# A graph network's second pass over its edge counts, with six chunk buffers in place of four

## The reference, cut to what matters

```
def sage_conv(x, edge_index, w_l, b_l, w_r):
    src, dst = (edge_index[0], edge_index[1])
    n = x.shape[0]
    msg_sum = jax.ops.segment_sum(x[src], dst, num_segments=n)
    deg = jax.ops.segment_sum(jnp.ones((src.shape[0],), x.dtype), dst, num_segments=n)
    mean = msg_sum / jnp.maximum(deg, 1.0)[:, None]
    return mean @ w_l + b_l + x @ w_r
h = jax.nn.relu(sage_conv(x, edge_index, w1_l, b1, w1_r))
return sage_conv(h, edge_index, w2_l, b2, w2_r)
```

## Time and profile before

| | |
|---|---|
| time, median of 3 runs | 5765.54 us (5760.69 to 5777.83) |
| span of the profiled execution | 5738.2 us |
| TensorE matmul busy | 3339.7 us (58%) |
| VectorE busy | 3535.7 us (62%) |
| TensorE mean granted clock | 0.733 of full |
| first row of `l1a_end` to first row of `l1b_end` on VectorE | 2585.84 to 2773.69 us |

### The profile page before, as it was taken

One profiled execution on the slowest core, in us unless ns is written; L12 is line 12 of the kernel. 1 busy time (PEld: TensorE's weight loads), 2 busy tenths in 40 slices (PEclk: granted clock), 3 DMA queues, 4 the chain that ended last, 5 costly groups with the idle time before them and its releaser, 6 DMA issues. The chain is left out here.

```text
span 5738.2 us, 59061 instructions
## 1 busy us (share of the span) xinstructions
PE 3339.7 (58%) x14332; PEld 2164.9 (38%) x14332; DVE 3535.7 (62%) x6569; ACT 2184.6 (38%) x3989; POOL 2244.9 (39%) x2086
## 2 busy tenths in 40 slices
PE   5666679999999999798413433325014342433564
PEld 3555534444444444355312323324013232323452
DVE  6999989999999999510214323325135553645676
ACT  4999968887878787300000000000002111111310
POOL 0000023333333333100276777773566666666200
PEclk8999989999999999899655555555555555555556
DMA  2555544444444443697411242210211111111011
GB/s 71 163 163 162 162 134 118 114 118 108 124 104 114 119 109 100 134 195 157 93 37 39 47 90 50 47 45 18 36 28 36 31 36 30 35 31 29 5 38 35
DMA packets 546254, 474.36 MB, mean 83 GB/s; under 512 B 185773, under 2 KB 439736, under 8 KB 545085
## 3 DMA queue, kind: packets, MB, share of 16 engines
q1 hardware_dynamic: 493723, 416.13, 28.6%
q0 software_dynamic: 52288, 55.34, 4.8%
HBM read 351.39 MB, written 119.84 MB: 82 GB/s over the span
## 5 line engine op out<-in xcount | busy, mean ns | idle before, releaser
L813 PE MATMUL l_sum_ps<-arena,sums 125*65 125x500 f32 (+1 forms) x2600 | 1140.8, 577 | 9.9 <-ACT arena L774 4.8
L1711 POOL DMA_INDIRECT l_rows<-table,tile_src x782 | 794.4, 1016 | 406.9 <-issue 212.0
L1126 POOL DMA_INDIRECT l_rows<-hidden_rows,tile_src x782 | 796.3, 1018 | 326.4 <-issue 231.8
L692 POOL COPY arena<-arena 125x750 f32<-125x750 f32 (+1 forms) x400 | 540.4, 1355 | 893.8 <-PE l_count_ps L802 855.7
L758 ACT ACTIVATE arena<-arena,far_left 125x750 f32<-125x750 f32 (+1 forms) x800 | 713.4, 939 | 282.7 <-DVE arena L711 282.7
L711 DVE SCALAR_TENSOR_TENSOR arena<-arena,far_past 125x750 f32<-125x750 f32 (+1 forms) x800 | 803.8, 1045 | 16.5 <-DMA arena<-score_rows 16.5
L722 DVE SCALAR_TENSOR_TENSOR arena<-arena,l_count_ps 125x750 f32<-125x750 f32 (+1 forms) x800 | 735.4, 960 | 96.5 <-ACT arena L763 51.9
L1187 PE MATMUL l_sum_ps<-l_rows,l_hot 128*125 x1612 | 359.9, 414 | 747.0 <-issue 678.7
L1153 DVE TENSOR_TENSOR sums<-sums,l_sum_ps 125x64 f32 x806 | 178.5, 222 | 744.4 <-DMA arena<-counts 527.5
L1187 PEld LDWEIGHTS l_sum_ps<-l_rows,l_hot 128*125 128x125 f32 x1612 | 341.3, 323 | 765.9 <-issue 765.3
L763 ACT ACTIVATE arena<-arena 125x1500 f32<-125x1500 f32 (+1 forms) x400 | 596.1, 1491 | 0.0
(11 more groups left out here) (438 smaller groups left out, 3032.3 us busy)
## 6 DMA issues: line engine op xcount, KB each, us to landing
arena<-counts SPq DMA_DIRECT2D x300, 328.1 KB
counts<-arena SPq DMA_DIRECT2D x324, 284.4 KB
arena<-counts SPq DMA_DIRECT2D x21, 2843.8 KB
arena<-counts SPq DMA_DIRECT2D x100, 382.8 KB
l_attr<-edge_attr_in SPq DMA_DIRECT2D x97, 256.0 KB
arena<-score_rows SPq DMA_DIRECT2D x24, 732.4 KB
l_rows<-hidden_rows,tile_src POOLq DMA_INDIRECT x782
l_rows<-table,tile_src POOLq DMA_INDIRECT x782
```

What stands on the lines that cost most here:

```text
L692: g.tensor_copy(laid[k % 2][:, 0:n * P].rearrange("p (b v d) -> p b v d", b=n, d=D), raw[k % RAWS][:, 0:n * P].rearrange("p (v b d) -> p b ...
L813: last = nc.tensor.matmul(sum_ps[0:F + 1, c, 0:hi - lo], h_one[:, w, :], z[k % ZS][:, lo:hi], start=(w == 0), stop=(w == W - 1))
L1126: pool.indirect_dma_start(rows[:, b % RING, t, :], None, m.hidden_rows[:, :], bass.IndirectOffsetOnAxis(ap=m.tile_src[:, k:k + 1], axis=0) ...
L1711: pool.indirect_dma_start(rows[:, t % RING3, :], None, m.table3[:, :], bass.IndirectOffsetOnAxis(ap=m.tile_src[:, t:t + 1], axis=0)).then_ ...
```

## The change

Two more buffers, `counts_extra0` and `counts_extra1` (`EXTRA = 2`), exist during `l1a_end` and `l1b`. In turn 1 the load of chunk `c` waits for the product of chunk `c - 6`. The load of chunk 4 goes into `counts_extra0` and is issued by SP in `l1a_end`; the load of chunk 5 goes into `counts_extra1` and is issued at the start of `l1b` without a wait. `cat` and `dense_sb` of `l1a_end` lie inside `counts_extra1`, which is why chunk 5 isn't loaded any earlier. The scratch of the layer norm, with its two semaphores, is made for kind "last" alone, the only one that uses it.

```diff
+EXTRA = 2
...
-        for i, x in enumerate(self.loads):
-            self.buffer[x] = i % HELD
+        for x in range(n):
+            self.buffer[x] = x % HELD
         for x in range(n, n + HELD):
             self.buffer[x] = self.buffer[x - HELD]
+        for x in range(n + HELD, n + HELD + EXTRA):
+            self.buffer[x] = x - n
+        for x in range(n + HELD + EXTRA, 2 * n):
+            self.buffer[x] = self.buffer[x - HELD - EXTRA]
...
-        self.counts_in = [stack.enter_context(nc.semaphore(f"counts_in{i}")) for i in range(HELD)]
+        self.counts_in = [stack.enter_context(nc.semaphore(f"counts_in{i}")) for i in range(HELD + EXTRA)]
+
+    def grow(self, nc, stack):
+
+        each = AT_ONCE * V // W * CW
+        extra = [stack.enter_context(nc.sbuf_tensor(f"counts_extra{i}", [128, each], F32)) for i in range(EXTRA)]
+        self.sb += [x[0:P, :].rearrange("p (v c) -> p v c", c=CW) for x in extra]
+        self.spare = extra[-1]
+
+    def room(self, turn_no):
+        return HELD + EXTRA * turn_no
...
         @block.sync
         def _(sp):
+            room = held.room(turn_no)
             for c, x in enumerate(order):
                 if c == HELD and tiles:
                     tiles.sp(sp)
-                if c >= HELD:
-                    sp.wait_ge(sums_ready, c - HELD + 1)
-                if x in held.loads and x >= EARLY:
+                if c >= room:
+                    sp.wait_ge(sums_ready, c - room + 1)
+                if x in held.loads and (c >= EARLY if turn_no == 0 else c >= room - 1):
                     held.load(sp, x)
...
-    def __init__(self, nc, s, m, ps_t, ps_o, tag):
+    def __init__(self, nc, s, m, ps_t, ps_o, tag, room=None):
...
-        self.turned_sb = s.sb(f"{tag}_sb", [128, W * P])
+        self.turned_sb = s.sb(f"{tag}_sb", [128, W * P]) if room is None else room
...
-        norm_scratch(s)
-        cat = s.sb("cat", [P, W, 2 * F])
+        if kind == "last":
+            norm_scratch(s)
+        if kind == "hidden":
+            spare = m.held.spare
+            cat, room = spare[0:P, 0:W * 2 * F].rearrange("p (w f) -> p w f", w=W), spare[:, W * 2 * F:W * 2 * F + W * P]
+        else:
+            cat, room = s.sb("cat", [P, W, 2 * F]), None
...
+        if kind == "hidden":
+            @block.sync
+            def _(sp):
+                for c in range(HELD, HELD + EXTRA - 1):
+                    m.held.load(sp, m.held.first[1] + c)
...
-                finish_mean(nc, m, "l1a_end", m.sage1[:, :], m.rows[:, 0:F], "hidden")
-                count_sum(nc, m, "l1b", 1)
+                with ExitStack() as extra:
+                    m.held.grow(nc, extra)
+                    finish_mean(nc, m, "l1a_end", m.sage1[:, :], m.rows[:, 0:F], "hidden")
+                    count_sum(nc, m, "l1b", 1)
```

More of the change, by code:

```diff
@@ L1272, in finish_mean @@
         ps_o = [s.ps(f"ps_o{i}") for i in range(4)]
-        dense = Dense(nc, s, m, ps_t, ps_o, "dense")
+        dense = Dense(nc, s, m, ps_t, ps_o, "dense", room)
         own_sem, rows_ready, written = s.sem("dve_step"), s.sem("rows_ready"), s.sem("written")
```

## The result

| | before | after |
|---|---|---|
| time, median of 10 runs | 5762.75 us (5750.19 to 5777.83) | 5741.82 us (5733.85 to 5751.09) |
| ratio | | 0.9958, 95% interval 0.9947 to 0.9969 |
| span of the profiled execution | 5738.2 us | 5739.2 us |
| `l1a_end` and `l1b`, first row to first row of `l1b_end` | 187.85 us | 165.21 us |

The two medians lie 20.9 us apart, 0.36%. The ratio, which is not the quotient of the two medians, says 0.42%, or 24.2 us, with an interval of 17.9 to 30.5 us. The forecast was 5742.1 us, 23.4 us less.

The account below looks back on a forecast made before the run. Loads were taken to bound `l1b` once under way. Waits of 15.8 us, slow products 6.6 and about 1 us of transposes made 23.4 us; 5765.5 less that gave 5742.1 us, range 5733 to 5754.

Parts of the forecast that it names:

- What bounds the pass: In `l1b`, loads are the tighter resource once under way: 15.5 us each against 11.0 of TensorE's work; six waits, 15.8 us.
- The load in the dense end costs nothing: In `l1a_end`, the load of chunk 4 beside the stage's own operations was costed at nothing; dense end 20.6 us as before.
- The landings, two chunks on: In `l1b`, chunk 12 lands when chunk 10 did, at 2733.71 us, with 3.5 us to spare.
- The sum: The pass ends at 2748.3 us instead of 2771.7, 23.4 us less: waits 15.8, slow products 6.6, the last us transposes.
- the sign of 11.06 us and clock 1.00 for all 13 chunks: In the profile after, all 13 chunks of `l1b` run at 11.06 us and clock 1.00, none at 12.7 or more.
- The time: Whole kernel: the timed median 5765.5 us less 23.4 gives 5742.1 us, 0.41% less.
- The slow products: In `l1b`, products after long waits took 12.73, 13.66 and 13.31 us, 6.6 over 11.06 each in all; to vanish with the waits.
- How the span stands to the time: The profiled span, 27.3 us under the timed median, was left so and forecast to go from 5738.2 to 5714.8 us.
- The page's rule: For loads in `l1b`, 358 GB/s plus 2 us gives 11.1 us a load, so six buffers gain about 0.
- Loads still the bound: Rival in `l1b`: with 18 us a load TensorE still waits 10 us; gain 9.2 us, time 5756.3; chance 0.12.
- No gain in the loads: Rival in `l1b`: the waits come from SP's issue or a buffer's release, not the transfers; time 5765; chance 0.05.
- Slower by held-up code: Rival at the barrier before `l1b`: a code-fetch stall could be longer beside a load in flight; slower given chance 0.03.

Follow-up runs that it names:

- e4: The kernel before with no loads in `l1b`, the four held chunks multiplied again, against the kernel before: 5728.4 us, ratio 0.9950.
- e6: The change with chunk 4 loaded twice into its buffer in the dense end, against the kernel before: 5612.2 us, ratio 0.9968.
- e1: Five buffers, the load of chunk 4 at the head of `l1b`, none in the dense end, against the kernel before: 5619.9 us, ratio 0.9971.
- e3: The change's extra buffers and smaller scratch with the loads left as before, against the kernel before: 5753.5 us, ratio 0.9992.
- a2: The whole change run again, against the kernel before in session C: 5726.6 us, ratio 0.9941.
- b2: The kernel before, unchanged, run again in session C for its trace: 5760.2 us, `l1a_end` and `l1b` 187.1 us.
- b3: The kernel before, unchanged, traced a third time, in session D: `l1a_end` and `l1b` 189.4 us.
- e5: Five buffers, the load of chunk 4 in the dense end, which works in its own memory, against the kernel before: 5623.4 us, ratio 0.9979.

## Why the prediction was right, point by point

*What bounds the pass.* Right. Six waits for loads and the slow products after them were all but 1 us of what lay between the kernel and TensorE's own time; e4 shows that floor at the change's time.

*The load in the dense end costs nothing.* Nearly. The dense end took 21.0 us in the first trace of the change in place of 20.6. From the first row of `l1a_end` to the first product it was 22.87 and 22.62 us, against 22.49 and 22.36 before. Sessions B and D had 22.40 in before, 22.33 in e6 and 22.34 in e1, so the difference is within what executions differ by. Nor is it tied to the load: e3, with nothing loaded in its dense end, had 20.9 and 22.78 us. The load took from 2588.89 to about 2605.1 us, 16.2 us; 15.5 to 16.6 was forecast.

*The landings, two chunks on.* Right, and this was the step that carried the result. Chunk 12 was to land 125.4 us after the first product (2733.7 less 2608.3) with 3.5 us to spare. The queue fell silent 125.7 us after it (2737.5 less 2611.8), with 3.6 to spare. The seven loads from that of chunk 6 on took 16.0 us each, under the 16.6 from which they would have decided. That the landing came within 0.3 us is in part luck: in a2 the queue fell silent 123.6 us after the first product, and in the other traces with the loads of before chunk 10 started 123.7 (b2), 125.9 (e3) and 127.1 us (b3) after it, where the prediction took the 125.4 of one trace. e6 then ate the spare time and gave back some 8 us.

*The sum.* 23.4 us was forecast; the stretch gave 22.6 in the first pair of traces and 22.4 in that of session C. Of the 0.8 missing in the first pair, half is the 0.4 of the dense end and half chunks 0 and 1, which took 24.21 us in place of 23.77. So the sign of 11.06 us and clock 1.00 for all 13 chunks was too strict for the first, before and after alike. TensorE comes out of the dense end's idle time with a lower clock (0.85 on average over chunk 0 in the trace of before, so part of it at 1.2 GHz), and how long that lasts differs from one execution to the next: the two chunks took 23.36 to 24.85 us over all traces. The timed interval, 17.9 to 30.5 us, holds all of these.

*The time.* 5741.8 us against 5742.1 is closer than the method is, and that is luck. The forecast started from the median of three runs of before, 5765.5 us; with ten runs that median is 2.8 us lower, and the medians differ by 20.9 us and not by 23.4.

*The slow products.* Right. They went with the waits, and they come back with them: 13.41 us after 4.21 in e1, 13.73 after 3.64 in e6. Not every wait brings one: in b3 a product took 12.73 us after 1.78 and another 11.11 after 3.19.

*How the span stands to the time.* This was the step that was read wrongly, though the sum didn't hang on it. The prediction left 27.3 us "as it is" between the profiled execution and the median of the runs, and forecast a span of 5714.8. After the change each timed run is shown with its span, and the two differ by 1.7 to 1.8 us (5740.95 and 5739.2 in the profiled one). If the same holds for before, its profiled execution took about 5740 us (an estimate), less than any of its ten timed runs (5750.2 at the least); it was short in `l2` and behind it. Its span had to be held against its own time; the forecast of a span from one such execution was off by 24 us.

*The page's rule.* The Trainium skill, in SBUF — State Buffer (Summary: rules for kernel authors), reckons 358 GB/s between HBM and SBUF. The runs here don't agree: over eight or nine loads in a row a load of 3.25 MB took 15.4 us (b2) to 16.3 us (e5), about 200 to 210 GB/s. The forecast by the rows came true, and that by the page, no gain, did not.

*The rivals.* Loads still the bound: not seen, with 16.0 us a load in the changed pass. No gain in the loads: refuted by the changed pass, whose waits are gone, together with e3, which has the same memory and keeps them. Slower by held-up code: refuted at this barrier by e6.

## What to carry to other kernels

When loads are tied to the work that frees their buffers, one more buffer moves every landing by one step, and the new landing times can be read off the old trace: this gave the gain within 1 us here, and the last landing within 2 us in both traces of the change. An earlier load pays only together with the buffer that keeps the queue busy behind it; e5 loaded 20 us earlier than e1 and gained less. And judge a change of 20 us by the stretch that it touches, cut at the same rows in both traces, never by the two spans.

## What the runs showed of the hardware that was not expected

- The stage `l2` takes 1079 to 1083 us in all eight traces of sessions B and D and 1161 to 1177 in the six of A and C, for the same instructions, while `l1b_end` takes 44.1 to 44.9 us in all fourteen. The median of before is 5632.1 us in B and 5760.2 in C. That is 2.2%, five times the effect studied here, so only runs of one session can be compared. B, C and D were run on three chips; whether the chip or something else of the session makes the difference is not shown.
- A load doesn't end sharply. At the end of the changed pass its last 2.7 us move at 26 to 69 GB/s, and where the next load is issued only as the one before it ends, as in e1, the rate dips to 31 GB/s at the handover.
- Eight loads behind an empty queue took 130.6 us and at most 131.5 in e5 and its repeat, against 126.1 to 129.0 elsewhere. The cause stays open.
